# Cross-scan layers: the softplus difference on TensorE, new places for the softplus steps, and copies issued by ScalarE

## What is computed

```
xin, z  = split(x @ in_proj.T)                       # 192 channels each
xs      = 4 orders of the 1024 positions: rows, columns, and both reversed
dt,B,C  = split(x_proj @ xs)                         # rank 12, 16 states, 16 states, per order
delta   = softplus(dt_proj @ dt + bias)              # 192 channels
h[t]    = exp(delta[t]*A) * h[t-1] + delta[t]*u[t]*B[t]      # 192 channels x 16 states
y[t]    = sum over states of h[t]*C[t]  + D*u[t]
out     = out_proj @ (layernorm(sum of the 4 orders' y) * silu(z))
```

## Time and profile before

| | us |
|---|---|
| median of 3 runs | 3563.06 (3560.85 to 3566.3) |
| the profiled execution, its own time | 3562.11 |
| its span, first to last instruction | 3560.3 |
| mean granted TensorE clock | 0.792 of full |

### The profile page before, as it was taken

The page is one execution under the profiler, slowest core; times in us unless marked ns, Lnnn a source line. Parts: engine busy times, 40 slices in busy tenths (PEclk is TensorE's granted clock), DMA queues, the critical chain, the costliest instruction groups (busy, mean ns, idle before and its releaser), DMA issues. The chain is left out here.

```text
span 3560.3 us, 27492 instructions
## 1 busy us (share of the span) xinstructions
PE 2462.7 (69%) x5948; PEld 618.4 (17%) x5948; DVE 2978.8 (84%) x1934; ACT 2042.1 (57%) x2262; POOL 2819.5 (79%) x1212
## 2 busy tenths in 40 slices
PE   5777677777677677335677776766777676767676
PEld 2111111111111111111111112111111111111111
DVE  1799999999989898675989841998999898999995
ACT  3566565757566665304655524756675656657573
POOL 0899999999999998003666622999999999999995
PEclk9777786888788877667788778768887888779787
DMA  1656556574755465103442502664737555655654
GB/s 42 159 137 152 133 142 149 126 171 111 178 136 142 121 154 126 30 0 90 122 108 78 122 7 68 148 161 124 170 104 177 136 142 132 154 132 145 150 125 106
DMA packets 140881, 437.19 MB, mean 123 GB/s; under 512 B 33909, under 2 KB 34619, under 8 KB 140395
## 3 DMA queue, kind: packets, MB, share of 16 engines
q1 hardware_dynamic: 140714, 435.58, 51.2%
HBM read 307.56 MB, written 6.82 MB: 88 GB/s over the span
## 5 line engine op out<-in xcount | busy, mean ns | idle before, releaser
L885 POOL TENSOR_TENSOR L_read<-L_state,L_c_rows 128x1024 f32<-128x1024 f32 x768 | 1795.2, 2358 | 79.6 <-DVE L_state L993 76.5
L671 PE MATMUL L_y_ps<-L_read,L_fold 128*64 128x512 f32 x3072 | 1027.8, 765 | 450.0 <-POOL L_read L885 448.1
L818 ACT ACTIVATE L_work_ps<-L_delta,L_a_neg 128x1024 f32<-128x1024 f32 x256 | 286.3, 1118 | 592.4 <-DVE L_state L993 592.3
L872 POOL TENSOR_TENSOR L_state<-L_du,L_b_rows 128x1024 f32<-128x1024 f32 x256 | 603.6, 2358 | 26.9 <-POOL L_read L885 4.2
L993 DVE TENSOR_TENSOR_SCAN L_state<-L_decay,L_work_ps 128x1024 f32<-128x1024 f32 x256 | 585.3, 2286 | 26.7 <-DVE L_work_ps L974 2.5
L993 DVE TENSOR_TENSOR_SCAN L_state<-L_work_ps,L_state 128x1024 f32<-128x1024 f32 x256 | 581.0, 2269 | 22.8 <-POOL L_state L872 21.8
L818 ACT ACTIVATE L_decay<-L_delta,L_a_neg 128x1024 f32<-128x1024 f32 x512 | 584.3, 1141 | 15.1 <-DVE L_state L993 10.1
L993 DVE TENSOR_TENSOR_SCAN L_state<-L_decay,L_row_ps 128x1024 f32<-128x1024 f32 x256 | 585.4, 2287 | 8.8
L974 DVE TENSOR_TENSOR L_work_ps<-L_du,L_row_ps 128x1024 f32<-128x1024 f32 x256 | 314.3, 1228 | 200.2 <-issue 147.0
L671 PEld LDWEIGHTS L_y_ps<-L_read,L_fold 128*64 128x64 f32 x3072 | 182.6, 157 | 1201.6 <-POOL L_read L885 912.2
L1523 POOL TENSOR_TENSOR L_read<-L_state,L_c_rows 128x1024 f32<-128x1024 f32 x96 | 237.7, 2476 | 164.8 <-DVE L_state L1629 140.0
(11 more groups left out here) (324 smaller groups left out, 2896.4 us busy)
## 6 DMA issues: line engine op xcount, KB each, us to landing
L_b_rows<-L_bc_dram SPq DMA_DIRECT2D x580, 256.0 KB, 4.2
L_c_rows<-L_bc_dram SPq DMA_DIRECT2D x580, 256.0 KB, 4.1
L_delta<-L_delta SPq DMA_DIRECT2D x204, 256.0 KB, 6.0
L_du<-L_du SPq DMA_DIRECT2D x140, 256.0 KB, 6.2
L_du<-L_u SPq DMA_DIRECT2D x64, 256.0 KB, 6.1
L_bc_dram<-L_dbl SPq DMA_DIRECT2D x40, 128.0 KB, 3.5
L_delta<-L_delta_a SPq DMA_DIRECT2D x16, 256.0 KB, 4.4
L_du<-L_du_a SPq DMA_DIRECT2D x16, 256.0 KB, 5.0
```

The source lines that it names most:

```text
L671: m = nc.tensor.matmul(y_to(c, o, i), fold[:, :], y_half(t, o, i), start=first, stop=last, skip_group_check=True)
L818: nc.scalar.activation(to[:, :], delta2[:, d * NBLK + c, :], ACT.Exp, scale=a_neg[:, o * 2 + d, c, p:p + 1]).then_inc(decay_ready, 1)
L872: nc.gpsimd.tensor_tensor(state[:, last, :], du2[:, d * NBLK + last, :], b_rows[:, g % 2, :], ALU.mult).then_inc(injected_c, 1)
L885: nc.gpsimd.tensor_tensor(read[:, t % READS, :], state[:, t % STATES, :], c_rows[:, g % 2, :], ALU.mult).then_inc(multiplied, 1)
```

## The change

In the turns (not in a layer's head, which is ahead of its first turn) the difference more - l is formed by PE: a new side "gap" of two halves, each two products (identity times `more`, minus identity times l) into `side_ps`, and ACT takes each half with Relu into l. POOL's gap (1024 positions, L857) and ACT's relu step (1024 positions, L775) go from the turns. The sum side now waits for the taking of the gap's second half. The places of sides and softplus steps are set anew; both halves of a sum stand at neighbouring tiles where there were two tiles between them before. The next turn's u sides of r = 1 start at tile 0 rather than 3.

The copies of delta and du (`copy_block`) of the turns go from SP's program to ACT's, after all other work of a tile: blocks 3, 4, 5 at tiles 3, 6, 9 and blocks 0, 1, 2 at tiles 38, 41, 44 (r = 0) or 32, 35, 38 (r = 1). The waits ahead of them are the same: `y_added` before the first of each three, `delta_ready` before each block. The head's three blocks stay with SP.

```
--- before.py
+++ after.py
@@ -311,27 +311,26 @@
 
 
 
-FINISH = [{("cent", 0): (1, 3), ("cent", 1): (4,), ("var", 0): (10, 11), ("out", 0): (15, 16)},
+FINISH = [{("cent", 0): (1, 3), ("cent", 1): (4,), ("var", 0): (10, 11), ("out", 0): (14, 15)},
           {("z", 0): (36, 37), ("z", 1): (38, 39), ("shift", 0): (43, 44)}]
-PREPARE = [{("u", 0): (6, 7), ("u", 1): (8, 9), ("bc", 0): (12, 13), ("dt", 0): (17, 18), ("dt", 1): (20, 21),
-            ("dt", 2): (23, 24), ("u", 2): (25, 26), ("sum", 0): (28, 30), ("sum", 1): (33, 35), ("sum", 2): (38, 40)},
-           {("u", 0): (3, 4), ("u", 1): (5, 6), ("bc", 0): (8, 9), ("dt", 0): (11, 12), ("dt", 1): (14, 15),
-            ("dt", 2): (17, 18), ("u", 2): (19, 20), ("sum", 0): (22, 24), ("sum", 1): (27, 29), ("sum", 2): (32, 34)}]
-ACT_SOFTPLUS = [{("exp", 0): 23, ("log", 0): 24, ("one", 0): 25, ("less", 0): 26, ("relu", 0): 28, ("exp", 1): 29,
-                 ("log", 1): 30, ("one", 1): 31, ("less", 1): 32, ("relu", 1): 34, ("exp", 2): 35, ("log", 2): 36,
-                 ("one", 2): 37, ("less", 2): 38, ("relu", 2): 40},
-                {("exp", 0): 17, ("log", 0): 18, ("one", 0): 19, ("less", 0): 20, ("relu", 0): 23, ("exp", 1): 24,
-                 ("log", 1): 25, ("one", 1): 26, ("less", 1): 27, ("relu", 1): 29, ("exp", 2): 30, ("log", 2): 31,
-                 ("one", 2): 32, ("less", 2): 33, ("relu", 2): 35}]
-POOL_GAP = [{24: 0, 30: 1, 36: 2}, {18: 0, 25: 1, 31: 2}]
-ACT_SIDES = ("u", "bc", "dt", "sum", "z", "cent", "var")
+PREPARE = [{("u", 0): (6, 7), ("u", 1): (8, 9), ("bc", 0): (12, 13), ("dt", 0): (16, 17), ("dt", 1): (19, 20),
+            ("dt", 2): (22, 23), ("u", 2): (25, 26), ("gap", 0): (27, 28), ("sum", 0): (30, 31), ("gap", 1): (32, 33),
+            ("sum", 1): (36, 37), ("gap", 2): (38, 39), ("sum", 2): (42, 43)},
+           {("u", 0): (0, 1), ("u", 1): (2, 3), ("bc", 0): (5, 6), ("dt", 0): (8, 9), ("dt", 1): (11, 12),
+            ("dt", 2): (14, 15), ("u", 2): (17, 18), ("gap", 0): (19, 20), ("sum", 0): (22, 23), ("gap", 1): (24, 25),
+            ("sum", 1): (28, 29), ("gap", 2): (30, 31), ("sum", 2): (34, 35)}]
+ACT_SOFTPLUS = [{("exp", 0): 22, ("log", 0): 25, ("one", 0): 28, ("less", 0): 29, ("exp", 1): 31, ("log", 1): 32,
+                 ("one", 1): 33, ("less", 1): 34, ("exp", 2): 35, ("log", 2): 37, ("one", 2): 38, ("less", 2): 39},
+                {("exp", 0): 14, ("log", 0): 17, ("one", 0): 20, ("less", 0): 21, ("exp", 1): 23, ("log", 1): 24,
+                 ("one", 1): 25, ("less", 1): 26, ("exp", 2): 27, ("log", 2): 29, ("one", 2): 30, ("less", 2): 31}]
+ACT_SIDES = ("u", "bc", "dt", "gap", "sum", "z", "cent", "var")
 SILU_AT, RSTD_AT, Y_AT, ADD_AT = 43, 16, 1, 21
 SKIP_AT = (1, 2, 3)
 CROSS_SKIP_AT = (2, 3, 4)
 FILL, FILL_FIRST = 1, 2
 FILL_AFTER = {(("var", 0), 1): 0, (("out", 0), 0): 0, (("out", 0), 1): 0, (("sum", 2), 1): 0,
               (("sum", 1), 0): 0}
-COPY_BELOW, COPY_ABOVE = (1, 2, 3), ((13, 13, 14), (11, 11, 12))
+COPY_BELOW, COPY_ABOVE = (3, 6, 9), ((38, 41, 44), (32, 35, 38))
 
 
 def side_uses(r, finish):
@@ -340,7 +339,7 @@
     return sorted((t, key, i) for key, ts in table.items() for i, t in enumerate(ts))
 
 
-HEAD_SIDES = side_uses(1, False)
+HEAD_SIDES = [s for s in side_uses(1, False) if s[1][0] != "gap"]
 TAIL_SIDES = [s for s in side_uses(0, True) if s[1] in FINISH[0]]
 
 
@@ -563,17 +562,6 @@
                         load_c(turn.next * GROUPS, turn.next_order, 0)
                     if g == GROUPS // 2:
                         store_bc(turn)
-                    if g == COPY_BELOW[0]:
-
-                        sp.wait_ge(y_added, number * NT + SUM0)
-                    if g in COPY_BELOW:
-                        copy_block(number, NBLK + COPY_BELOW.index(g))
-                    if g == COPY_ABOVE[turn.r][0]:
-
-                        sp.wait_ge(y_added, turn.next * NT - NT // 2 + SUM0)
-                    for q, at in enumerate(COPY_ABOVE[turn.r]):
-                        if g == at:
-                            copy_block(turn.next, q)
 
             store_bc(Head())
             load_b(0, 0, 0, 0)
@@ -612,8 +600,15 @@
                 elif kind == "dt":
                     wait_side(pe, turn.use(("bc", 0), 1))
                     parts = [(w_dt[:, turn.next_order, j * 128:(j + 1) * 128], dbl[:, s])]
+                elif kind == "gap":
+                    pe.wait_ge(sp_log, turn.next * NJ + j + 1)
+                    pe.wait_ge(sp_less, turn.next * NJ + j + 1)
+                    parts = [(ident, more[:, s]), (minus_w[:, :], l_of[j][:, s])]
                 elif kind == "sum":
-                    pe.wait_ge(sp_relu, turn.next * NJ + j + 1)
+                    if isinstance(turn, Head):
+                        pe.wait_ge(sp_relu, j + 1)
+                    else:
+                        wait_side(pe, turn.use(("gap", j), 1))
                     parts = [(ident, e_of[j][:, s]), (minus_w[:, :], l_of[j][:, s]), (ident, delta[:, j, s])]
                 elif kind == "z":
                     parts = [(w_z[:, j * 128:(j + 1) * 128], g_half(turn.done_image, i))]
@@ -728,6 +723,8 @@
                     bias = dt_bias[:, turn.next_order, j:j + 1]
                     nc.scalar.activation(e_of[j][:, s], side_ps[:, :], ACT.Abs, bias=bias).then_inc(sp_abs, 1)
                     ins = nc.scalar.activation(delta[:, j, s], side_ps[:, :], ACT.Relu, bias=bias)
+                elif kind == "gap":
+                    ins = nc.scalar.activation(l_of[j][:, s], side_ps[:, :], ACT.Relu)
                 elif kind == "sum":
                     if not isinstance(turn, Head):
                         act.wait_ge(sp_du, 2 * (turn.next * NJ + j) + i + 1 - NJ)
@@ -764,8 +761,10 @@
                     nc.scalar.activation(l[:, :], e[:, :], ACT.Ln, bias=1.0).then_inc(sp_log, 1)
                 elif kind == "one":
                     act.wait_ge(sp_exp, n + 1)
-                    if j > 0 or not isinstance(turn, Head):
-                        act.wait_ge(sp_gap, n)
+                    if j > 0 and isinstance(turn, Head):
+                        act.wait_ge(sp_gap, j)
+                    elif j > 0:
+                        act.wait_ge(side_ready, turn.use(("gap", j - 1), 1) + 1)
                     nc.scalar.activation(more[:, :], e[:, :], ACT.Identity, bias=1.0).then_inc(sp_one, 1)
                 elif kind == "less":
                     act.wait_ge(sp_one, n + 1)
@@ -773,6 +772,15 @@
                 else:
                     act.wait_ge(sp_gap, n + 1)
                     nc.scalar.activation(l[:, :], l[:, :], ACT.Relu).then_inc(sp_relu, 1)
+
+            def copy_block(n, q):
+                j, half = q // 2, q % 2
+                rows = slice(half * BLK, half * BLK + BLK)
+                act.wait_ge(delta_ready, n * NJ + j + 1)
+                for side in range(2):
+                    to = slice(side * BLK, side * BLK + BLK)
+                    act.dma_start(delta2[to, q, :], delta[rows, j, :]).then_inc(delta2_in[q], 16)
+                    act.dma_start(du2[to, q, :], du[j][rows, :]).then_inc(du2_in[q], 16)
 
             def silu(turn):
 
@@ -829,6 +837,14 @@
                     for (kind, j), at in ACT_SOFTPLUS[o].items():
                         if at == t:
                             softplus(turn, kind, j)
+                    if t == COPY_BELOW[0]:
+                        act.wait_ge(y_added, number * NT + SUM0)
+                    if t in COPY_BELOW:
+                        copy_block(number, NBLK + COPY_BELOW.index(t))
+                    if t == COPY_ABOVE[o][0]:
+                        act.wait_ge(y_added, turn.next * NT - NT // 2 + SUM0)
+                    if t in COPY_ABOVE[o]:
+                        copy_block(turn.next, COPY_ABOVE[o].index(t))
 
             ahead = {0: (("exp", 0), ("log", 0), ("one", 0), ("less", 0), ("exp", 1), ("log", 1), ("relu", 0), ("one", 1),
                          ("less", 1)),
@@ -849,10 +865,9 @@
 
         @block.gpsimd
         def _(pool):
-            def gap(turn, j):
-                n = turn.next * NJ + j
-                pool.wait_ge(sp_log, n + 1)
-                pool.wait_ge(sp_less, n + 1)
+            def head_gap(j):
+                pool.wait_ge(sp_log, j + 1)
+                pool.wait_ge(sp_less, j + 1)
                 l = l_of[j]
                 nc.gpsimd.tensor_tensor(l[:, :], more[:, :], l[:, :], ALU.subtract).then_inc(sp_gap, 1)
 
@@ -886,18 +901,16 @@
                                             ALU.mult).then_inc(multiplied, 1)
                     if turn.r == 0 and turn.finish and t == ADD_AT:
                         add_x(turn)
-                    if t in POOL_GAP[turn.r]:
-                        gap(turn, POOL_GAP[turn.r][t])
 
             def form_du(j):
 
                 wait_side(pool, Head().use(("sum", j), 1))
                 nc.gpsimd.tensor_tensor(du[j], delta[:, j, :], u[:, j, :], ALU.mult).then_inc(sp_du, 1)
 
-            gap(Head(), 0)
-            gap(Head(), 1)
```

(4 more changed lines are left out.)

## The result

The changed kernel takes 3592.45 us (median of 10 runs, 3575.09 to 3602.5); the kernel before took 3566.35 us in the runs beside it (10 runs, 3560.85 to 3573.9). The ratio is 1.007, with a 95% interval of 1.0054 to 1.0086: slower by 26 us. The forecast was 3511 us and faster. The profiled execution of the changed kernel took 3600.47 us, at the upper end of its runs, and its span is 3598.3 us; so the two traces differ by 38 us where the medians differ by 26.

The account below looks back on a forecast made before the run. POOL and DVE were level but neither full, so DVE's waits, mostly for PE and ACT, were to be cut. Gains of 19, 43 and 20 us less a cost of 30 made -52 us: 3511 us, range 3460 to 3600.

Parts of the forecast that it names:

- Part 2: Sums at new places: DVE's waits for PE fall from 81 to 38 us, a gain of 43 us.
- Part 3: Copies leave SP: B loads no longer stand behind blocks, gaining 20 of DVE's 41.9 us of waits for B rows.
- Part 4: Copies issued by ACT: blocks of 3.6 us delay some B-row copies, costing 30 us.
- Part 1: The difference leaves POOL: DVE's waits for POOL's inject fall from 21.8 to 3 us, a gain of 19 us.
- first rival: ACT's block issue waits for queued decays or takes turns with SP's DMAs: slower, 3607 us, up to 3690; chance 0.22.
- third rival: DVE's waits for PE stay at 81 us, first halves at half clock and second halves late: 3554 us; chance 0.10.
- The second: Blocks on ACT cost nothing, its queue being empty at each: 3481 us; chance 0.20.
- the fourth: The DMA engines are the limit, B rows late whoever issues, the 20 us don't come: 3531 us; chance 0.08.

Follow-up runs that it names:

- e7: Changed kernel with the copies back on SP at their old groups and the halves of five of six sums two tiles apart: 3497.46 us, ratio 0.9799.
- e11: e7 with six unread products per turn added on GpSimd (POOL), about where the differences were before: 3559.23 us, ratio 0.998.
- e4: Changed kernel with the halves of five of the six sums two tiles apart again, gaps 1 and 2 a tile later: 3548.86 us, ratio 0.9953.
- e8: Changed kernel with three products by a zero matrix added on PE ahead of each second half of a sum in the turns: 3564.86 us, ratio 0.999.
- e9: e6 with dt sides and last finishing side of r = 0 at their old tiles, two softplus steps of r = 1 at middle tiles: 3469.58 us, ratio 0.9729.
- e6: Changed kernel with ACT's copy blocks at the groups' middle tiles and the halves of five of six sums two tiles apart: 3498.65 us, ratio 0.9804.
- e2: Kernel before with only the copies moved to ACT, at the changed kernel's tiles: 3596.74 us, ratio 1.0079.
- e1: Changed kernel with the copies of delta and du back on SP at their old groups: 3571.89 us, ratio 1.0013.
- e12: Kernel before with only the copies moved to ACT, at the groups' middle tiles: 3552.48 us, ratio 0.9968.
- e10: e7 with dt sides and last finishing side of r = 0 at their old tiles, two softplus steps of r = 1 at middle tiles: 3480.07 us, ratio 0.9765.
- e5: Changed kernel with copy blocks still on ACT but at the groups' middle tiles, lower ones a tile later, upper a tile earlier: 3565.51 us, ratio 0.999.

## Why the prediction was wrong

It was 81 us too low, and it had the sign wrong. DVE's idle time in the turns, 223 us where 142 were forecast, has the same 81, and by its own steps 42 of them are Part 2, 33 Parts 3 and 4, less 3 of Part 1; the other 9 are the longer waits for finishing sides, which the sum does not have. The measured time lies inside the stated range, but near its upper end (3600), which stood for a part of the first rival; that rival's mechanism is not what happened, so this is luck.

**Part 1** held in what it priced: the waits for POOL's inject went from 21.8 us to none (forecast 3), POOL's busy time per turn to 149.8 us (149 to 152), L900's and L887's durations didn't move, and POOL's reads wait for DVE's scans (210.3 of their 218.9 us) and hardly for the y matmuls behind the gaps. Its sentence that POOL's relief is "worth those 22 us at most" is not borne out in e7's order: e11 puts 94.5 us of work back, fewer than the 113 removed, and loses 62, with 3.8 us of direct waits for POOL. A row of waits for an engine counts only those that wait for it directly.

**Part 2** is the step that failed: 38 us of waits for PE were forecast, 80.3 came. The first halves did what it says. They are early, and the one exception, the first sum of r = 0, has a wait of 1.0 us in the mean of eight turns, inside the 0 to 1.1 given (1.7 at most). The mis-sized term is the second half, "ACT's copy 0.59, PE 2.84, and some 0.2": the 2.84 us were read in the earlier trace rows, where PE had just worked and had the full clock. Two tiles apart, PE did y products between the halves, and in before's trace it idled for 0.3 us at most ahead of a second half. One tile apart it idles for 0.4 to 3.9 us while it waits for the take, and 27 of 48 times it then ran in part at the half clock: 4.1 to 5.5 us, and a wait of 1.4 to 3.6 in place of 0 to 0.9. The 21 that kept the full clock made waits of 0 to 0.7 us, as forecast. The forecast's terms for second halves come to 8 x (0.9 + 2.4) = 26 us; the trace has 72, of which the half clock is 49 by the estimate above and 23 would be left. So the step is the full clock in "PE 2.84", and the rest of the term came near (23 against 26). The prediction took the half clock into account for the first halves, where an idle stretch preceded, and not for the second, to which the change itself brought one. This is the third rival's outcome (PE's waits stay at 81 us), though it argued mostly from first halves; e4 (44 us) and e8 (28 us, what the added products cost deducted) show it.

**Part 3** held at its main place: the wait at group 15 of r = 0 is gone, as were all of ACT's waits for B loads. But of the 41.9 us it was to leave 22 of ACT's own lateness, and there are 45: the change moved dt sides and softplus steps next to row copies with 1.1 us of slack, which the prediction did not cost at all. e9, which moves some of them, shows it for the dt sides: the waits at tiles 21, 24 and 27 of r = 0 (14.3 us in e6) are gone.

**Part 4** had the block right: 2.8 to 4.3 us each, 3.4 in the mean against 3.6 taken, its first two DMAs at 0.47 and 0.65 us in the mean, and its issue beside a running activation (the rows at 918.12). The upper blocks of r = 0 cost a mean of 0.8 us behind tile 38 (forecast 1.4), 0.9 behind tile 41 (0.4) and nothing behind tile 44; those of r = 1 cost 2 us in all. What failed is "at tiles 3, 6, 9 ... no wait". The step counted two queued decays ahead of the block and left out the take of the u side, which waits for PE: 2.7 us at tile 6 of r = 1, in 8 turns 22 of the 40 us behind blocks. Of this kind is the 0.4 us that it gave to tile 3, the right idea at the wrong tile. The place in the program decides, and the five pairs show it:

```
copies on ACT, against the same kernel with them on SP (us)
at the change's tiles:      e2 - before  +31     after - e1  +21
at the groups' middle tile: e12 - before -12     e6 - e7      +1     e9 - e10  -10
```

**The rivals.** The first, an issue that is serial with the activations or takes turns with SP's, gave the right sign but is not what happens (its upper price, 1.9 us for each of 96 blocks, should read 3693 and not 3690): decay and block start together at 918.12, and a block on ACT takes no longer than it did on SP (3.4 us in the mean against 3.75 before). The Trainium skill's lock on the block that generates descriptors (Perfetto Trace Analysis, "DMA Instruction — HWDGE (DVE, Sync)") leaves hardly a mark on ACT's blocks: at 1038.61 SP issues two row DMAs in the middle of one, which still takes 3.6 us, and the 70 of 96 blocks with a DMA of SP's in them take 3.40 us in the mean, the other 26 take 3.34. SP's row DMAs do show something: the 141 issues that overlap one of ACT's take 0.82 us in the mean, the other 875 take 0.53. Whether that is the lock or a fuller queue was not tried. The second (blocks cost nothing) falls with e5, whose move of the blocks alone gave 27 us back; the fourth (the B rows are late whoever issues) with the changed kernel's own trace, in which ACT never waits for a B load.

**What stays open.** In e1 the three rows of waits that changed most (for PE, the B rows and POOL's inject) give 9 us less than before, and the kernel is 6 us slower. Its trace accounts for that: in the turns DVE is idle for 199 us against 194, with 6 us of new waits for a finishing side (x_cm), 4 more at L_sq_b and 6 ahead of the first injects of two turns. The part of L_sq_b goes in e9 and e10, where the last finishing side is at its old tiles (26.4 to 22.4 us); for the other two no run moves what causes them. Whether POOL's relief is worth in before's order what it is worth in e7's was not tried.

## What to carry to other kernels

A DMA issue of 256 KB cost its engine's sequencer 0.5 to 2.1 us here, and a block of four 2.8 to 4.3; it belongs behind the last instruction of that engine which is due soon, and not behind one that may wait. When two dependent steps share a buffer and are moved closer, the producer's work between them goes too: on TensorE the second step is then to be priced at the half clock as well (27 of 48 here), from a row that has an idle stretch ahead of it. And the waits for an engine in a profile were no bound on what its relief is worth (3.8 us of waits beside 62 us in e11), where loads are released by it.

## What the runs showed of the chip

The mean granted clock of TensorE rose with the change from 0.792 to 0.835 of its full 2.4 GHz (PE is busy for 1995 us of the turns in place of 1888), and yet 27 of the 48 halves that matter ran in part at 1.2 GHz. The mean says nothing on the clock of the one product that is waited for, and neither does the idle stretch ahead of it alone: at tile 32 of r = 1 PE had idled for 3.2 us in two turns, and the granted clock of the half was 0.62 in one and 1.00 in the other.

Added products of TensorE, none of them used, took 28 us off the kernel (e8), with a mean clock of 0.845.

The kernels with the halves next to each other spread wide from run to run (after 3575 to 3602 us, e1 3564 to 3581, e5 3546 to 3576), and e4 (3547 to 3552), e7 (3496 to 3498) and e6 (3491 to 3505), with the halves apart, less. But e11 has them apart too and spreads from 3551 to 3573, and so does before, 3556 to 3579. What goes with the spread is how many halves ran in part at the half clock in the trace: 27, 37 and 33 second halves in after, e1 and e5, ten in e11 and 43 first halves in before, against one in e4 and e8 (3558 to 3570) and none in e6 and e7. That fits halves which get the full clock in some runs and not in others; but there is one trace of each, and fewer runs of the quiet ones (five against ten and more), so it is not shown.
